# Layer 0 of a four-layer graph network: the key comparisons move to VectorE and read SBUF, and the late stores are spread out

## The reference

```
x = _layernorm(x + _L0_gnn_ref(x, src, dst, edge_weight, L0_gnn_weight, L0_gnn_bias), axis=-1)
x = _layernorm(x + _L1_gnn_ref(...), axis=-1)
x = _layernorm(x + _L2_gnn_ref(...), axis=-1)
x = _layernorm(x + _L3_gnn_ref(...), axis=-1)
```

```
gathered = edge_weight[:, None] * x[edge_col]
neigh = segment_sum(gathered, edge_row, num_segments=N_NODES)
out = x @ w_self + neigh @ w_neigh + bias
```

## Time and profile before

| | us |
|---|---|
| median of 3 runs | 3588.87 |
| lowest and highest | 3582.74, 3589.08 |
| the profiled execution's own time | 3576.91 |
| its span | 3575.1 |
| busy in the span: PE, DVE, ACT, POOL | 2961.2, 2435.7, 1527.0, 1683.7 |

### The profile page before, as it was taken

How to read it: one execution, slowest core, us unless ns; L and a number is a source line. 1 busy time by engine, 2 the same in 40 slices (tenths; PEclk the granted TensorE clock), 3 DMA queues, 4 the chain that set the end, 5 groups by cost and what they waited for, 6 DMA issues and landing times. The chain is left out here.

```text
span 3575.1 us, 59355 instructions
## 1 busy us (share of the span) xinstructions
PE 2961.2 (83%) x15273; PEld 1895.3 (53%) x15274; DVE 2435.7 (68%) x5480; ACT 1527.0 (43%) x3125; POOL 1683.7 (47%) x1731
## 2 busy tenths in 40 slices
PE   5789999989999598978769976776986569999996
PEld 2235444667777344467644434553443357587675
DVE  8895333568888898954789976569985763343444
ACT  1452222379998366631046655004654440310402
POOL 2777773046555766205777771576777300000000
PEclk6899999999999799978979997798998679999998
DMA  7998888378998365356721110993445233133241
GB/s 311 343 347 311 314 297 299 116 236 257 268 270 263 114 192 166 107 210 215 226 63 28 27 27 7 312 302 105 128 133 182 66 103 122 50 122 99 85 135 36
DMA packets 392781, 625.09 MB, mean 175 GB/s; under 512 B 129011, under 2 KB 274100, under 8 KB 385486
## 3 DMA queue, kind: packets, MB, share of 16 engines
q1 hardware_dynamic: 254085, 427.07, 36.4%
q0 software_dynamic: 72144, 145.54, 13.8%
q10 hardware_dynamic: 66365, 50.39, 4.3%
HBM read 442.67 MB, written 183.69 MB: 175 GB/s over the span
## 5 line engine op out<-in xcount | busy, mean ns | idle before, releaser
L1526 ACT ACTIVATE onehot<-iota,drel 128x128 f32<-128x128 f32 x1248 | 381.7, 388 | 684.8 <-PE ps L1231 345.1
L1231 PE MATMUL ps<-shared_sb,onehot 128*128 128x264 f32 (+1 forms) x1600 | 552.0, 441 | 93.2 <-DVE accum L2322 88.3
L2322 DVE TENSOR_TENSOR accum<-accum,ps 128x264 f32 (+1 forms) x1248 | 528.2, 423 | 10.6 <-DVE accum L2322 4.0
L1231 PEld LDWEIGHTS ps<-shared_sb,onehot 128*128 128x128 f32 x1600 | 259.4, 199 | 384.8 <-issue 239.6
L790 POOL DMA_INDIRECT t_w<-early_sb x391 | 379.6, 971 | 172.3 <-issue 94.0
L807 POOL TENSOR_SCALAR onehot<-iota,carry_d 98x512 bf16<-98x512 f32 x28 | 44.7, 1601 | 783.1 <-PE ps L1308 645.7
L1291 PE MATMUL ps<-counts_r,h_hi 128*128 128x512 f32 (+1 forms) x1050 | 322.1, 388 | 12.2 <-DVE h_lo L2584 12.2
L826 POOL DMA_INDIRECT shared_sb<-table,src_x x272 | 259.2, 953 | 115.1 <-issue 76.3
L1291 PE MATMUL ps<-counts_r,h_lo 128*128 128x512 f32 (+1 forms) x1050 | 313.0, 379 | 0.0
L826 POOL DMA_INDIRECT rows<-table,src_x x184 | 179.4, 975 | 176.5 <-DMA table<-score_sb 92.0
L873 POOL DMA_INDIRECT resid_sb<-table,src_x x224 | 211.6, 944 | 89.2 <-issue 57.7
(11 more groups left out here) (438 smaller groups left out, 6031.1 us busy)
## 6 DMA issues: line engine op xcount, KB each, us to landing
t_w<-onehot SPq DMA_DIRECT2D x13, 6400.0 KB
accum<-t_hot SPq DMA_DIRECT2D x208, 256.0 KB
shared_sb<-t_adj SPq DMA_DIRECT2D x53, 640.0 KB, 9.9
resid_sb<-t_w SPq DMA_DIRECT2D x13, 1664.0 KB
t_aside<-rows POOLq DMA_DIRECT2D x40, 512.0 KB
resid_sb<-t_w SPq DMA_DIRECT2D x13, 1536.0 KB
score_sb<-t_w SPq DMA_DIRECT2D x12, 1664.0 KB
shared_sb<-t_w SPq DMA_DIRECT2D x12, 1536.0 KB
```

What stands on the lines that cost most here:

```text
L1231: pe.matmul(ps[:, RING[(HU * h + u) % len(RING)], 0:w], onehot[:, h % 2 * HU + u, :], around[g][place(g, i, h)][:, u, 0:w], start=True, st ...
L1526: last = act.activation(onehot[:, h % 2 * HU + u, :], iota[:, 0:P], ACT.Abs, bias=drel[:, bass.ds(step + u, 1)], scale=-1.0)
L2322: dve.tensor_tensor(to, to, bank.unsqueeze(1), ALU.add).then_inc(step_acc, 1)
```

## The change

ScalarE no longer compares. It copies each key row from PSUM to one of four rows in SBUF (`key_row`), and VectorE makes all 4 x 98 comparisons from there. TensorE's PSUM bank is free once the copy is done (`key_sb`). There are two slots for the marks, as VectorE had before. The first loads of ScalarE's queue are issued one by one at quads 16, 20, 24, 28, 32 and 36. SP calls `step_rows_out` after loop step 4 instead of 6, waits for its stores at step 7, and issues the 27 copies in five parts, behind the zeros of steps 7 to 11.

```diff
+        key_row = [resid_sb[:, 2176 + r * EB * P:2176 + (r + 1) * EB * P] for r in range(4)]
...
-                sp.wait_ge(*count("rows_out", 64))
+
+            def low_rows_out(these):
+
                 by_steps = t_lo.rearrange("n (j r) e -> (n j) r e", j=QU)
-                for i in range(S // UN + 1):
+                for i in these:
...
-                if n == PIECES // 2:
+                if n == 4:
                     step_rows_out()
+                if n == 7:
+                    sp.wait_ge(*count("rows_out", 64))
+                if 7 <= n < 12:
+                    low_rows_out(range((S // UN + 1) * (n - 7) // 5, (S // UN + 1) * (n - 6) // 5))
...
                 if k >= 4:
-                    pe.wait_ge(*compared(k - 4))
+                    pe.wait_ge(*count("key_sb", k - 3))
...
-                pe.wait_ge(*compared(k))
+                pe.wait_ge(*count("same_dve", k + 1))
...
-            def compare(k):
+            def copy_row(k):

                 act.wait_ge(*count("key_ps", k + 1))
-                if k >= SHARE:
-                    act.wait_ge(*count("quad_sum", slot_before(k) + 1))
-                    act.wait_ge(*count("same_act", k // SHARE))
-                for u in range(L0H):
-                    at = k * L0H + u
-                    act.activation(key_gap[:, u, :], ps[:, k % 4, :], ACT.Abs, bias=adj_f[:, at:at + 1], scale=-1.0).then_inc(done("key_used"), 1)
-                act.wait_ge(*count("key_used", L0H * (k // SHARE) + L0H))
-                act.activation(same_slot(k)[:, :, :], key_gap[:, :, :], ACT.Relu, bias=ones[:, 0:1], scale=-1.0).then_inc(done("same_act"), 1)
+                if k >= 4:
+                    act.wait_ge(*count("same_dve", k - 3))
+                act.activation(key_row[k % 4], ps[:, k % 4, :], ACT.Copy).then_inc(done("key_sb"), 1)
...
+                elif k == 32:
+                    act.dma_start(cols[:, :, :], a["x_cols"].rearrange("(c p) n -> p c n", p=P)).then_inc(done("ld_x"), 16)
+                elif k == 36:
+                    act.dma_start(hrows[:, :, 0:D], a["x_pad"].rearrange("(t p) d -> p t d", p=P)).then_inc(done("ld_xh"), 16)
+                copy_row(k)
...
-                dve.wait_ge(*count("key_ps", k + 1))
-                if slot_before(k) >= 0:
-                    dve.wait_ge(*count("quad_sum", slot_before(k) + 1))
+                dve.wait_ge(*count("key_sb", k + 1))
+                if k >= 2:
+                    dve.wait_ge(*count("quad_sum", k - 1))
                 for u in range(L0H):
-                    last = dve.tensor_scalar(same_slot(k)[:, u, :], ps[:, k % 4, :], adj_f[:, k * L0H + u:k * L0H + u + 1], None, ALU.is_equal)
+                    last = dve.tensor_scalar(same_key[k % 2][:, u, :], key_row[k % 4], adj_f[:, k * L0H + u:k * L0H + u + 1], None, ALU.is_equal)
...
-                    if not on_act(k):
-                        compare(k)
+                    compare(k)
```

More of the change, by code:

```diff
@@ L48 @@
 QUADS = ET // L0H
-SHARE = 4
 BATCHES = [2, 2, 4] + [8] * 11 + [2]
@@ L226, in build @@
         values = flat_a[:, 2048:2832].bitcast(BF16).rearrange("p (j v) -> p j v", v=4)
-        same_key = [buf.bitcast(BF16).rearrange("p (u e) -> p u e", u=L0H) for buf in (shared_sb[:, 3200:4224], flat_a[:, 2880:3904], resid_sb[:, 5248:6272])]
+        same_key = [buf.bitcast(BF16).rearrange("p (u e) -> p u e", u=L0H) for buf in (shared_sb[:, 3200:4224], flat_a[:, 2880:3904])]
         tiles_le = flat_a[0:EQ, 4096:4096 + EB * NT].rearrange("p (b t) -> p b t", b=EB)
@@ L252, in build @@
         pick_row = over("pick_row", "resid_sb", 5120, [P])
-        key_gap = flat_a[:, 4224:4224 + 2 * L0H * P].bitcast(BF16).rearrange("p (u e) -> p u e", u=L0H)
+        key_row = [resid_sb[:, 2176 + r * EB * P:2176 + (r + 1) * EB * P] for r in range(4)]
         ring = {"gcn": shared_sb[:, 0:HOLD * GRP * CW // 2].bitcast(F16).rearrange("p (r c w) -> p r c w", r=HOLD, c=GRP)}
@@ L347, in build @@
                   [(f"{n}{k}", c) for k in (1, 2) for n, c in (("gat_in", NC), ("self_sub", 1), ("gat_out", NG))] + [("elu2", NC)],
-                  [("weighted1", 2), ("self_w1", 1), ("weighted2", 2), ("self_w2", 1)], [("diag_clear", 1), ("apart", S // QU), ("gaps", 3 * (S // HU))], [("x1_back", 16), ("x2_back", 16)], [("quad_sum", QUADS), ("own_mm", NT), ("adj_turned", BLOCKS * PAIRS)], [("same_act", QUADS // SHARE), ("adj_staged", BLOCKS * PAIRS)], [("w_summed", QUADS), ("own_sum", NT)], [("step_mask", EB), ("te", 1), ("adj_rows", 1), ("key_parts", 1), ("adj_ev", 1), ("keys", 2), ("pre", 1), ("attr_split", 1)], [("te_ps", 3), ("adj_tp", 1), ("steps_ps", 2), ("steps_ev", 1), ("early_one", 1)],
+                  [("weighted1", 2), ("self_w1", 1), ("weighted2", 2), ("self_w2", 1)], [("key_sb", QUADS), ("diag_clear", 1), ("apart", S // QU), ("gaps", 3 * (S // HU))], [("x1_back", 16), ("x2_back", 16)], [("quad_sum", QUADS), ("own_mm", NT), ("adj_turned", BLOCKS * PAIRS)], [("adj_staged", BLOCKS * PAIRS)], [("w_summed", QUADS), ("own_sum", NT)], [("step_mask", EB), ("te", 1), ("adj_rows", 1), ("key_parts", 1), ("adj_ev", 1), ("keys", 2), ("pre", 1), ("attr_split", 1)], [("te_ps", 3), ("adj_tp", 1), ("steps_ps", 2), ("steps_ev", 1), ("early_one", 1)],
                   [("p0_" + n, c) for n, c in parts], [("rest_" + n, c) for n, c in in_three],
@@ L404, in counts_landed @@
             return adj_in[at % LAND], kept_before[at % LAND] + 16 * before
[L406 to L420, removed]
         def first_lap(i):
@@ L1008, in marks @@
                 for b in range(L0H):
-                    mm = pe.matmul(ps[0:32, 4 + n % 2, :], spread_v[n % 2][:, b * WIDE + kk * 32:b * WIDE + kk * 32 + 32], same_slot(k)[:, b, :],
+                    mm = pe.matmul(ps[0:32, 4 + n % 2, :], spread_v[n % 2][:, b * WIDE + kk * 32:b * WIDE + kk * 32 + 32], same_key[k % 2][:, b, :],
                                    start=(kk == 0 and b == 0), stop=(kk == BATCHES[n] - 1 and b == L0H - 1))
@@ L1449, in _ @@
+                act.activation(key_row[k % 4], ps[:, k % 4, :], ACT.Copy).then_inc(done("key_sb"), 1)
             for k in range(QUADS):
                 if k == 16:
-                    first_loads()
-                if on_act(k):
-                    compare(k)
+                    act.wait_ge(*count("attr_split", 1))
+                    act.wait_ge(*count("adj_ev", 1))
+                    act.dma_start(t_attr.rearrange("(b q) e -> q b e", b=SB), attr_b.rearrange("p b m e -> p b (m e)")).then_inc(done("attr_out"), 16)
+                elif k == 20:
+                    act.dma_start(rows[:, :, :], a["rows"]).then_inc(done("ld_rows"), 16)
+                elif k == 24:
+                    act.dma_start(vecs[:, :, :], a["vecs"]).then_inc(done("ld_vecs"), 16)
+                elif k == 28:
+                    act.dma_start(weights[:, :, 0:D], a["L0_gnn_weight"].rearrange("(c p) n -> p c n", p=P)).then_inc(done("ld_w0"), 16)
+                elif k == 32:
+                    act.dma_start(cols[:, :, :], a["x_cols"].rearrange("(c p) n -> p c n", p=P)).then_inc(done("ld_x"), 16)
+                elif k == 36:
+                    act.dma_start(hrows[:, :, 0:D], a["x_pad"].rearrange("(t p) d -> p t d", p=P)).then_inc(done("ld_xh"), 16)
```

## The result

The changed kernel takes 3681.64 us (median of 4 runs, 3671.94 to 3690.95) against 3586.79 for the kernel before on the same chip: ratio 1.0267, 95% interval 1.0249 to 1.0284. The forecast was 3584.6 with a range from 3576 to 3632; the time lies 50 us above its upper end, on the side of the second rival, and past it. The profiled execution has a span of 3684.5 us.

The account below looks back on a forecast made before the run. Two chains, marks plus own products and zeros plus first load, were taken to bound the pair stage's start, with scatters close behind; -7.8 (stores) + 3.0 (clock) + 0.5 (POOL) = -4.3 us gave 3584.6 us, range 3576 to 3632.

Parts of the forecast that it names:

- the second rival: Scatters starve during the marks, each waiting 0.82 us for a quad's end; pair 11 loads 40.6 us later, 3629.5 us; chance 0.32.
- the chains: Marks plus own products, and zeros plus first load, end together at the first pair matmul (315.86); shortening the first alone gives nothing.
- The third chain: POOL's 391 scatters from 77.3 to 581.5 us, whose last group pair 11 needs; 17.4 us to spare.
- the marks: Comparisons before the pair stage, from SBUF at 0.41 us each: marks shorten by 34 us, end near 256, all slack.
- the stores: Late stores spread among the zeros on SP's queue: 7.8 us come back, first pair load near 296.4.
- TensorE's clock: At the pair stage's start, after idling from 281 to 308, half of 6 us lost: 3.0 us.
- POOL against VectorE: During the marks each scatter waits 0.15 us more for SBUF comparisons; scatters 13 us late, costing 0.5 us.
- The first rival: Scatters pass and TensorE's clock holds; pair stage starts 7.8 to 9.6 us earlier, 3579.3 us; chance 0.27.
- the third: Rival on the late stores: the five parts leave gaps, zeros end where they did, about +2 us; chance 0.08.

## Why the prediction was wrong, step by step

**Right: the chains.** Two chains end together at the first pair product; shortening either one alone can't be told from no change, and shortening both gives 10.4 us. The third chain, scatters, has 17.4 us to spare and then decides: 95 us by that sum, 98.5 in the trace.

**Right but mis-sized: the marks.** From SBUF a comparison was costed at 0.41 us, a quad at 1.64; they follow at 0.396 and 1.58. The marks end at 237.27 instead of 256. 11.6 of these 19 us were costed at nothing: the run with the loads alone shows what ScalarE's six issues ahead of its comparison had held up. The pitch gives 98 x 4 x 0.014 = 5.5 more. That the two add up in the kernel after is taken, not shown. ScalarE's copies are hidden, as forecast, and the 53 us by which the marks are shorter than before are all slack.

**Right but mis-sized: the stores.** The DMA share from 164 to 180 rises from 0.51 to 1.02, and alone they bring the first pair load 8.2 us forward (7.8 forecast). In the kernel after it came 15.7 us earlier; 8.9 of those remain with the stores put back, where only the comparisons and ScalarE's loads differ from before, and the loads alone bring 0.4 (303.81). The scatters that were not done there also took no share of the queues; that this is the 8.9 us is argued, not shown.

**Right: TensorE's clock.** Granted 0.51 from 262 to 300 us (1.2 GHz of 2.4) after the idle time; the first two products of pair 0 take 2.02 us, where two late in the pair stage of the kernel before take 1.13. The level is that of the earlier trace rows. 3.0 us were taken for it; the first block of pair 0 took 4.12 us (298.95 to 303.07) where the kernel before took 2.22 (315.86 to 318.08), so it cost 1.9, and that is lost behind the scatters.

**Wrong: POOL against VectorE.** The step that failed is "each scatter waits for the end of the comparison at hand, 0.20 us, in three cases of four". That is about true of runs of four with a pause behind them, 1175 and 1126 ns against the 1.11 us of the forecast (0.96 and 0.15), and not where VectorE never pauses: there the mean wait is 8029 - 958 = 7.1 us, 47 times as long. The row that showed it was read, the gather held 6.52 us to the end of 32 operations; it was set aside with "a quad's run is four operations, not 32, and with TensorE at 1.63 us a quad VectorE will often pause between them". VectorE doesn't pause. The four key rows let it run ahead: from 100 to 230 us TensorE and its weight loads waited 31.5 us in sum for VectorE's marks, and VectorE was never idle. A batch is 32 comparisons, with one copy and one reduce and cast out of PSUM among them that leave no idle moment, and most scatters left only with the copy. The second rival, which had 0.32, was the right mechanism with the wrong length of run: a quad's end, 0.82 us of wait, 3629.5, where it was mostly the batch's copy. Even so the 17.4 us of its threshold decided. The first rival had the scatters at 0.96 us throughout, and the third the first pair load still at 304; 8029 ns and 288.48 us rule both out.

By the rule that the prediction cited from the Trainium skill (SBUF — State Buffer, section "Who interferes with whom") the later one waits until the first instruction has finished. In the runs with a pause behind each quad most scatters agree, being over within 1.3 us; the kernel after doesn't: 13.33 us, where one comparison has 0.47. Between two back-to-back comparisons POOL mostly loses again there.

## What to carry to other kernels

A VectorE operation that becomes cheaper by reading SBUF can hold up POOL's indirect DMAs: before moving a back-to-back loop out of PSUM, look at what POOL does beside it and how long VectorE goes without an idle moment, not how long one call is. If the loop must stay, a wait for its own last result or a 0.15 us copy from PSUM behind every four instructions gives most of POOL back (96 and 95 of 106 scatters). And where several chains end together, price the change at the last of them: here 53 us off one chain was worth nothing, and 11 and 8 us off two were worth 10.

## What was not expected of the hardware

Back-to-back fp32 SBUF comparisons kept one indirect DMA's issue on POOL for 13.3 us, over some 32 instructions, and through a reduce and a cast from PSUM among them. A pause of some 35 ns behind every four is enough to avoid it, without any operation (96 scatters at 1126 ns). The fast form bought VectorE 0.73 - 0.47 = 0.26 us per comparison, and the same comparison with an accumulator output takes 731 ns, just what it took out of PSUM. What lets one scatter in between two comparisons and not the next remains open.
